# Key strips kept once per head, with zeros in the other heads' rows, for the scores of a causal attention stage

## The chip, the cores and the metric

The kernel runs on one NeuronCore of a Trainium2 chip. The metric is the device time of one execution in microseconds. PE is TensorE's matmuls, PEld its weight loads, DVE is VectorE, ACT is ScalarE, POOL is GpSimd, SP is SyncE.

## The reference

Four stages, each followed by a residual and a layer norm over 128 features, on x of 4 x 512 x 128 float32: a retention layer, two windowed attention layers with feed-forward, a causal attention layer, and a gated feed-forward of four matrix products. The change touches the causal stage alone:

```python
k = einsum('bte,fe->btf', x, Wk).reshape(B, T, 16, 8)    # q and v alike
k = layernorm(k, kln_g, kln_b); q = layernorm(q, qln_g, qln_b)   # over the 8 values of a head
dot = einsum('bihd,bjhd->bhij', q * s, k * s)
dot = where(causal, -inf, dot)
att = softmax(dot, axis=-1)
out = einsum('bhij,bjhd->bihd', att, v).reshape(B, T, 128)
return einsum('bte,fe->btf', out, Wo) + bo
```

## The kernel before, in words

All weights stay in SBUF. A hardware loop runs twice (`Fori(0, 2)`), and each turn does the four stages on two of the four sequences of 512 positions (8 tiles of 128 tokens; `G = 8`, `NT = 4`). Each engine has its own program, written out in order; semaphores join them, and nothing is planned at run time. PSUM's eight banks of 128 x 512 float32 are given out by `take`, which makes PE wait until the bank's last user is done.

**The causal stage.** A head has 8 values. Each of q and k is kept as a rounded high part and a low remainder, and these with two rows for the negated row maximum fill 32 slots for each head (`QS`, `KS`). Four heads make 128 slots. So the unit of work is `u`, 0 to 7: one of two sequences and one quad of heads. For each `u` PE transposes the four token tiles of `QS` and of `KS` (helper `transposes`, recorded at line 358) into bank 6, and ACT copies the bank out (helper `evac`, line 1227) as `qS[128, 512]` and `kS[128, 512]` in float32r: partition 32h + r is slot r of head h. These are the strips. `qS` and `qS2` have two buffers, `kS` has three.

- `first_pass` (line 628) makes scores with queries as the stationary operand: head n of pair p takes partitions 64p + 32n to + 32 of both operands, so a product contracts over 32 rows. Query tile t needs keys 0 to (t + 1) x 128. After the scores of two pairs, `masked` (line 615) adds the causal mask with a bf16 product of full width. DVE takes the row maxima of a bank pair (line 1114, `maxima`).
- `negated` writes the negated maxima into `QS`; PE transposes again, ACT copies to `qS2`. `second_pass` (line 647) makes transposed scores less the maximum, with keys as the stationary operand; ACT takes the exponential of a bank pair (line 1403), POOL clears the part above the diagonal (line 1575), and `values` (line 661) multiplies with v, 32 columns of the array for each head, into bank 7.
- `head_outputs` transposes the result (line 358), DVE divides (lines 1135, 1136), and later the output projection and layer norm follow (`finish`, line 682).

The stage is a loop over 24 steps and a tail (`for s in range(END)`). Step 3u + i makes group i of the first pass of unit `u` (`A_GROUPS`: 512 columns a head; 128 + 384; 256) and group i of the second pass four steps later (`B_GROUPS`, the same widths). A group has two fills, one for each pair of heads, and a fill takes one of three bank pairs. A fill of the second pass so waits for `maxima` to free its pair, or for the exponential. `k_strips(u + 1)` stands last in step 3u + 2, after `head_outputs`; step 3u + 3 opens with `first_pass` of unit u + 1, which waits for `kS_ready`. Both use bank 6.

`table2` holds the rotary tables of the windowed layers (2048 float32 for each partition). DVE writes it in `tables`, in the retention stage of each turn, and reads it last in the second windowed layer, where `swapped_ready` comes to 32.

**Ahead of the loop.** POOL waits for a DMA, casts a mask (line 1590), and enters the loop, where its first work is an addition over x (line 1498). ACT waits for `zeros_ready` and enters the loop, where its first work is the copy of the transposed x to `x_features`. PE's first products (line 376) need that copy.

Of the kernel before, what the change touches and what calls it, by code (L numbers as in the profile page):

```python
# [15 lines left out]
F32 = mybir.dt.float32  # L16
F32R = mybir.dt.float32r
# [4 lines left out]
P = 128  # L22
S = 512
NT = 4
G = 8
D = 128
H1, K1, V1 = 16, 8, 16
H2, D2, WIN = 8, 64, 64
# [37 lines left out]
def build(nc, x, wts, rows, consts, out):  # L66
    with ExitStack() as ctx:
        def sb(name, shape, dt=F32):
            return ctx.enter_context(nc.sbuf_tensor(name, shape, dt))

        def sem(name):
            return ctx.enter_context(nc.semaphore(name))
# [5 lines left out]
        xM = sb("x_tokens", [P, G, D])  # L78
        xi = sb("x_inner", [P, G, D])
        hT = sb("x_features", [P, 2, S + 1])  # L80
        table2 = sb("rotary2", [P, 2, 2, NT, 2, D2])
        band_bf = sb("band_bf", [P, 2, P], BF16)
        ident_bf = sb("ident_bf", [P, P], BF16)
        neghalf = sb("neghalf", [P, 1])
# [4 lines left out]

        qS = sb("q_strips", [P, 2, S], F32R)  # L90
        qS2 = sb("q_strips_shifted", [P, 2, S], F32R)
        kS = sb("k_strips", [P, 3, S], F32R)
        later_bf = sb("later_bf", [P, P], BF16)
        gb3 = sb("gain_bias3", [P, 512])
        neg3 = sb("negmax3", [P, 16], F32R)

        ARENA = 21200
        STAGING = 19600
        arena = sb("arena", [P, ARENA])

        def carve(sizes):
            offs, end = offsets(sizes)
            assert end <= ARENA, end
            return {k: arena[:, a:a + w] for k, (a, w) in offs.items()}
# [85 lines left out]
        psum = [banks[:, 512 * i:512 * i + 512] for i in range(8)]  # L190
# [9 lines left out]
        zeros_ready = sem("zeros_ready")  # L200
        masks_loaded = sem("masks_loaded")
        masks_ready = sem("masks_ready")
        arrived = sem("arrived")
        go = sem("go")
        settle = sem("settle")
# [3 lines left out]
        def counter(name):  # L209
            s = sem(name)  # L210
            cleared.append(s)
            return s
# [35 lines left out]
             "negmax_ready", "pe_qS2", "qS2_ready", "pe_B", "E_ready", "pe_V", "oS_ready", "pe_oS", "oN_ready",  # L248
             "pe_oN", "oNT_ready", "pe_wo3", "z3_ready"))
        xb3_ready = counter("xb3_ready")  # L250
        hi_placed = counter("hi_placed")
        kept3 = counter("kept3")

# [20 lines left out]
        def held(key):  # L274
            return psum[place[key]]
# [19 lines left out]
        A_GROUPS = [[(3, 0)], [(0, 0), (2, P)], [(1, 0)]]  # L295
# [6 lines left out]
        def fill_of(f):  # L302

            return f // NF, f % NF // 2, f % 2
# [50 lines left out]
        def _(pe):  # L355
# [217 lines left out]
            def causal():  # L573
# [32 lines left out]
                def next_pair(key, until):  # L606
                    i = filled[0] % 3
                    filled[0] += 1
                    for n in range(2):
                        take(pe, (key, n), until, bank=2 * i + n)  # L610
                    place[key] = i
                    return i
# [5 lines left out]
                def first_pass(fills):  # L618
                    for f in fills:
                        u, group, p = fill_of(f)  # L620
                        if f % NF == 0:
                            pe.wait_ge(qS_ready, u + 1)
                            pe.wait_ge(kS_ready, u + 1)
                        i = next_pair(("A", f), [(mx_ready, f + 1)])
                        for n in range(2):
                            rows = slice(64 * p + 32 * n, 64 * p + 32 * n + 32)
                            for t, at in A_GROUPS[group]:
                                pe.matmul(psum[2 * i + n][:, at:at + (t + 1) * P], qS[rows, u % 2, t * P:(t + 1) * P],  # L628
                                          kS[rows, u % 3, 0:(t + 1) * P], start=(at == 0), stop=False,
                                          skip_group_check=True)  # L630
                    for f in fills:
                        u, group, p = fill_of(f)
                        for n in range(2):
                            for t, at in A_GROUPS[group]:
                                mm = masked(psum[2 * place["A", f] + n], at + t * P)
                        mm.then_inc(pe_A, 1)

                def second_pass(fills):
                    for f in fills:
                        u, group, p = fill_of(f)  # L640
                        if f % NF == 0:
                            pe.wait_ge(qS2_ready, u + 1)
                        i = next_pair(("B", f), [(E_ready, f + 1)])
                        for n in range(2):
                            rows = slice(64 * p + 32 * n, 64 * p + 32 * n + 32)
                            for t, at in B_GROUPS[group]:
                                mm = pe.matmul(psum[2 * i + n][:, at:at + (NT - t) * P],  # L647
                                               kS[rows, u % 3, t * P:(t + 1) * P], qS2[rows, u % 2, t * P:S],
                                               start=(at == 0), stop=True, skip_group_check=True)
                        mm.then_inc(pe_B, 1)  # L650

# [39 lines left out]
                for s in range(END):  # L691
# [24 lines left out]
                    for k in HIDDEN_AT.get(s, ()):  # L716
                        i = filled[0] % 3
# [49 lines left out]
            with pe.Fori(0, 2) as it:  # L767
                retention()
                retention_end(pe)
                pe.wait_ge(consts_loaded[2], 16)  # L770
                pe.wait_ge(tables_ready, 1)
                for l in range(2):
                    pe.wait_ge(loaded[2 + l], 16)
                    if l == 0:
                        pe.wait_ge(pads_ready, 1)
                    window_layer(l)
                    gelu_layer(l)
                pe.wait_ge(strips_blank, 2)
                pe.wait_ge(masks_ready, 1)
                causal()  # L780
                mlp()
                pair_end(pe, it)
# [442 lines left out]
        def _(act):  # L1225
            def evac(dst, src):
                return act.activation(dst, src, ACT.Copy)  # L1227
# [124 lines left out]
            def causal():  # L1352
# [32 lines left out]
                def k_strips(u):  # L1385
                    act.wait_ge(pe_kS, u + 1)
                    if u >= 3:
                        act.wait_ge(pe_B, NF * (u - 2))
                    evac(kS[:, u % 3, :], held(("kS", u))[:]).then_inc(kS_ready, 1)

                def shifted_strips(u):
                    act.wait_ge(pe_qS2, u + 1)
# [61 lines left out]
            def mlp():  # L1454
# [17 lines left out]
            act.dma_start(C[:, CONST_CUTS[1]:CONST_CUTS[2]], consts[:, CONST_CUTS[1]:CONST_CUTS[2]])\  # L1472
                .then_inc(consts_loaded[1], 16)
            act.wait_ge(zeros_ready, 1)
            with act.Fori(0, 2) as it:
                retention()
                retention_end(act)
                act.wait_ge(pads_ready, 1)
                for l in range(2):
                    act.wait_ge(loaded[2 + l], 16)  # L1480
                    window_layer(l)
                    gelu_layer(l)
                causal()
                mlp()
                pair_end(act, it)
# [3 lines left out]
        def _(pool):  # L1489
# [66 lines left out]
                        root(LN2 + 2 * G + g)  # L1556

            def causal():
                pool.wait_ge(xM_ready, 2 * G)
                pool.tensor_tensor(xi[:], xM[:], r_("bo3").unsqueeze(1).to_broadcast([P, G, D]), ALU.add)\  # L1560
                    .then_inc(xb3_ready, 1)
                def affine(g):
                    pool.wait_ge(scaled3, g - NT + 1)
                    flat = cen3[:, g % NT].rearrange("p h d -> p (h d)")
                    pool.tensor_tensor(flat, flat, gb3[:, 0:256], ALU.mult).then_inc(affine_step, 1)
                    pool.wait_ge(affine_step, g - NT + 1)
                    pool.tensor_tensor(flat, flat, gb3[:, 256:512], ALU.add).then_inc(affine3, 1)

                def keep(f):

                    u, group, p = fill_of(f)
                    pool.wait_ge(E_ready, f + 1)
                    for t, at in B_GROUPS[group]:
                        diagonal = PT3[group][:, 2 * p:2 * p + 2, at:at + P]
                        ins = pool.affine_select(out=diagonal, in_=diagonal, pattern=[[0, 2], [1, P]],  # L1575
                                                 compare_op=ALU.is_ge, fill=0.0, base=0, channel_multiplier=-1)
                    ins.then_inc(kept3, 1)

                for s in range(END):
                    for g in SCALE_AT.get(s, ()):  # L1580
                        affine(g)
                    for f in fills_b(s):
                        keep(f)
                    if s in FINISHED_AT:
                        root(LN3 + FINISHED_AT[s])
                for g in range(NT, G):
                    root(LN3 + g)

            pool.wait_ge(masks_loaded, 16)
            pool.tensor_copy(later_bf[:],  # L1590
                             arena[:, STAGING:STAGING + MASKS_WIDTH]).then_inc(masks_ready, 1)
            pool.wait_ge(zeros_ready, 1)
            pool.wait_ge(rows_loaded[0], 16)
            with pool.Fori(0, 2) as it:
# [173 lines left out]
```

## Time and profile before

| | |
|---|---|
| median of 3 runs | 1305.03 us |
| the runs | 1286.44, 1307.96, 1305.03 us |
| profiled execution, its own time | 1297.12 us |
| span of the profiled execution | 1295.4 us |
| PE busy | 1031.7 us (80%) |
| DVE busy | 749.7 us (58%) |
| ACT busy | 542.9 us (42%) |
| POOL busy | 388.8 us (30%) |
| mean granted clock of TensorE | 0.856 |

The span is the time from the first to the last instruction of the profiled execution. Busy times are unions over an engine's instructions; the clock is a share of full speed, 1.0 being 2.4 GHz and 0.5 being 1.2 GHz.

### The profile page before, as it was taken

To read this page: it belongs to the slowest core of one execution; us is meant where nothing else is said; L and a number is where in the kernel's file an instruction comes from. 1 tells how busy PE (TensorE), PEld (TensorE's weight loads), DVE (VectorE), ACT (ScalarE), POOL (GpSimd) and SP (SyncE) were. 2 spreads that over 40 slices of the span, in tenths; PEclk is the share of its full clock that TensorE was granted. 3 is DMA by queue.
4 is the path that set the end of the run, shared out by engine and by line. 5 is a ranking of instruction groups with operands and counts; after the bars stand their busy time and mean duration, and the time that the engine had idled before them with its cause. 6 is when DMAs were issued, how large, how long until landed. Compare 5 with 4: busy or idle time off the path is not lost.

```text
span 1295.4 us, 18716 instructions
## 1 busy us (share of the span) xinstructions
PE 1031.7 (80%) x6640; PEld 638.7 (49%) x6640; DVE 749.7 (58%) x1906; ACT 542.9 (42%) x1066; POOL 388.8 (30%) x373
## 2 busy tenths in 40 slices
PE   6996688978884777899389957888788847877994
PEld 3665466645662444444246644566466523443443
DVE  4675578577867655330356746885887666443303
ACT  3730455445533554531065304553555335444410
POOL 2235445144441322200213444531443503122001
PEclk9876799989996698699787757999899956687997
DMA  8000000010000000000100001000100000000001
GB/s 334 2 1 0 22 17 22 1 25 13 22 1 1 1 2 1 1 1 1 34 2 1 1 1 25 18 18 1 25 22 14 1 1 1 2 1 1 1 1 32
DMA packets 11630, 21.61 MB, mean 17 GB/s; under 512 B 1424, under 2 KB 6928, under 8 KB 11024
## 3 DMA queue, kind: packets, MB, share of 16 engines
q1 hardware_dynamic: 11248, 18.60, 4.9%
q10 hardware_dynamic: 288, 1.79, 0.4%
q8 instruction: 56, 0.92, 0.3%
q14 instruction: 38, 0.31, 0.1%
HBM read 11.87 MB, written 1.05 MB: 10 GB/s over the span
## 4 chain that ended last, share of the span: by engine, by line
PE 64%; DVE 19%; issue 7%; ACT 5%; POOL 2%; POOLq 1%; DMA 1%; SPq 0%; DVEq 0%; ACTq 0%
PE bank L740 9%; PE bank L358 7%; PE bank L392 6%; PE bank L498 6%; PE bank L407 5%; PE bank L457 4%; PE bank L661 4%; DVE arena L1114 3%; PE bank L521 3%; PE bank L531 2%; DVE arena L970 2%; PE bank L730 2%; PE bank L628 2%; PE bank L647 2%; PE bank L492 2%
## 5 line engine op out<-in xcount | busy, mean ns | idle before, releaser
L1227 ACT ACTIVATE arena<-bank 128x512 f32<-128x512 f32 (+3 forms) x340 | 165.4, 528 | 263.5 <-PE bank L358 239.1
L358 PE MATMUL bank<-consts_sb,arena 128*128 128x128 f32 x960 | 154.0, 300 | 81.3 <-DVE arena L1106 26.7
L358 PEld LDWEIGHTS bank<-consts_sb,arena 128*128 128x128 f32 x960 | 116.4, 154 | 141.3 <-issue 57.6
L1114 DVE TENSOR_REDUCE arena<-bank 128x2 f32<-128x1024 f32 (+3 forms) x128 | 98.1, 819 | 105.3 <-PE bank L615 105.2
L1527 POOL TENSOR_TENSOR arena<-arena,neghalf 128x16 f32<-128x16 f32 x32 | 93.3, 2915 | 215.7 <-DVE arena L972 215.7
L1492 POOL TENSOR_TENSOR rstd<-vareps,neghalf 128x1 f32<-128x1 f32 x96 | 54.8, 571 | 260.1 <-DVE vareps L800 259.7
L1575 POOL TENSOR_SCALAR_AFFINE_SELECT arena<-arena 128x256 f32<-128x256 f32 x128 | 50.9, 411 | 226.5 <-ACT arena L1403 224.2
L740 PE MATMUL bank<-arena,weights 128*128 128x512 f32 x256 | 111.9, 594 | 1.6 <-ACT arena L1459 1.6
L457 PE MATMUL bank<-weights,x_features 128*128 128x512 f32 x192 | 94.2, 632 | 10.6 <-ACT x_features L1227 10.6
L1403 ACT ACTIVATE arena<-bank 128x1024 f32<-128x1024 f32 (+1 forms) x96 | 81.9, 881 | 48.7 <-PE bank L647 47.9
L392 PE MATMUL bank<-arena 128*128 128x512 f32 x128 | 79.1, 775 | 5.2 <-ACT arena L1251 5.1
L498 PE MATMUL bank<-arena 128*64 128x128 f32 x1024 | 78.2, 300 | 0.0
L740 PEld LDWEIGHTS bank<-arena,weights 128*128 128x128 f32 x256 | 48.0, 190 | 61.0 <-issue 57.4
L1251 ACT ACTIVATE arena<-arena,consts_sb 128x128 f32<-128x128 f32 x256 | 75.6, 396 | 0.0
L970 DVE TENSOR_REDUCE arena<-arena 128x16 f32<-128x1024 f32 x32 | 39.0, 1218 | 62.2 <-ACT arena L1285 62.2
L498 PEld LDWEIGHTS bank<-arena 128*64 128x64 f32 x1024 | 61.5, 150 | 17.2 <-issue 17.2
L407 PEld LDWEIGHTS bank<-arena 128*128 128x128 f32 x512 | 67.3, 212 | 3.2 <-issue 1.9
L1533 POOL TENSOR_TENSOR arena<-arena 128x1024 f32<-128x1024 f32 x28 | 66.0, 2357 | 0.0
L647 PE MATMUL bank<-q_strips_shifted,k_strips 32*128 32x512 f32 (+3 forms) x256 | 48.3, 450 | 22.1 <-DVE arena L1114 21.6
L407 PE MATMUL bank<-arena 128*128 128x17 f32 x512 | 65.6, 276 | 0.0
L1003 DVE TENSOR_REDUCE arena<-bank 128x4 f32<-128x512 f32 x64 | 44.0, 688 | 33.2 <-PE bank L498 31.5
L1459 ACT ACTIVATE arena<-bank,weights 128x512 f32<-128x512 f32 x32 | 22.0, 687 | 97.6 <-PE bank L740 97.6
(164 smaller groups left out, 1788.3 us busy)
## 6 DMA issues: line engine op xcount, KB each, us to landing
arena<-arena SPq DMA_DIRECT2D x56, 130.0 KB, 2.3
weights<-wts_dram SPq DMA_DIRECT2D x1, 2824.0 KB, 19.3
weights<-wts_dram SPq DMA_DIRECT2D x1, 1817.0 KB, 13.3
weights<-wts_dram SPq DMA_DIRECT2D x1, 1561.0 KB, 9.4
x_tokens<-x_dram SPq DMA_DIRECT2D x6, 256.0 KB, 3.0
consts_sb<-consts_dram ACTq DMA_DIRECT2D x1, 1232.5 KB, 7.1
out_dram<-x_inner SPq DMA_DIRECT2D x16, 64.0 KB, 1.5
consts_sb<-consts_dram SPq DMA_DIRECT2D x1, 768.0 KB, 4.6
```

The source lines that it names most:

```text
L358: mm = pe.transpose(bank[:, i * P:(i + 1) * P], src, ident)
L392: pe.matmul(bank[:], kT1[:, b, t * P:(t + 1) * P], qx1[g % 2][:, 4 * c:4 * c + 4, :], start=True, stop=True).then_inc(pe_sc, 1)
L407: mm = pe.matmul(bank[:, 17 * h:17 * h + 17], PT1[:, g % 2, h, :], v1[:, g, h, :], start=(t == 0 and h == 0), stop=(h == H1 - 1), skip_gro ...
L457: pe.matmul(bank[:], hT[:, b, t * P:(t + 1) * P], w_(f"qkv2_{l}")[:, 512 * j:512 * j + 512], start=True, stop=True).then_inc(done, 1)
L498: mm = pe.matmul(bank[64 * w:64 * w + 64, i * P:(i + 1) * P], qT2[:, g % 2, h // 2, 64 * w:64 * w + 64], kz[:, g % 2, h, 64 * w:64 * w + P ...
L647: mm = pe.matmul(psum[2 * i + n][:, at:at + (NT - t) * P], kS[rows, u % 3, t * P:(t + 1) * P], qS2[rows, u % 2, t * P:S], start=(at == 0), ...
L740: mm = pe.matmul(bank[:], w_(name)[:, 512 * c + k * P:512 * c + (k + 1) * P], src[:, b, c, :], start=(c == 0), stop=(c == 3))
L1114: ins = dve.tensor_reduce(mx3[:, u % 2, t, 2 * p:2 * p + 2], scores[:, :, at:at + (t + 1) * P], AX, ALU.max)
L1227: return act.activation(dst, src, ACT.Copy)
L1251: ins = act.activation(qx1[g % 2][:, h, :], qT1[:, b, t * P:(t + 1) * P], ACT.Copy, scale=c_("headmask")[:, h:h + 1])
L1403: act.activation(PT3[group][:, 2 * p:2 * p + 2, 0:wide], pair_view(place["B", f])[:, :, 0:wide], ACT.Exp).then_inc(E_ready, 1)
L1527: pool.tensor_tensor(rn2[:, g % 2, :], ss2[:, g % 2, :], neghalf[:].to_broadcast([P, 16]), ALU.pow).then_inc(rn_ready, 1)
```

## The change

The keys' strips are stored four times, `kS[128, 3, 4, 512]`. Copy h holds head h's 32 rows; the other 96 rows are zero. POOL clears buffers 0 and 1 once ahead of the loop and buffer 2 in each turn, since buffer 2 now lies on the memory of `table2`. ACT writes the copies with four activations of 32 partitions each instead of one of 128. Both passes then contract over all 128 rows: the query operand is the whole strip of four heads, and the zeros take the other heads out. In the first pass the loop over tiles is now the outer one and that over the two heads the inner one. The arena is 96 floats smaller.

```diff
-        kS = sb("k_strips", [P, 3, S], F32R)
+        at = nc.sbuf_base
+        kS = sb("k_strips", [P, 3, 4, S], F32R)
+        table2 = nc.alloc_sbuf_tensor_at("rotary2", [P, 2, 2, NT, 2, D2], F32, offset=at + 2 * 4 * S * 4)
...
                             pe.wait_ge(kS_ready, u + 1)
+                            if u == 2:
+                                pe.wait_ge(third_blank, 2)
                         i = next_pair(("A", f), [(mx_ready, f + 1)])
-                        for n in range(2):
-                            rows = slice(64 * p + 32 * n, 64 * p + 32 * n + 32)
-                            for t, at in A_GROUPS[group]:
-                                pe.matmul(psum[2 * i + n][:, at:at + (t + 1) * P], qS[rows, u % 2, t * P:(t + 1) * P],
-                                          kS[rows, u % 3, 0:(t + 1) * P], start=(at == 0), stop=False,
+                        for t, at in A_GROUPS[group]:
+                            for n in range(2):
+                                pe.matmul(psum[2 * i + n][:, at:at + (t + 1) * P], qS[:, u % 2, t * P:(t + 1) * P],
+                                          kS[:, u % 3, 2 * p + n, 0:(t + 1) * P], start=(at == 0), stop=False,
                                           skip_group_check=True)
...
                         for n in range(2):
-                            rows = slice(64 * p + 32 * n, 64 * p + 32 * n + 32)
                             for t, at in B_GROUPS[group]:
                                 mm = pe.matmul(psum[2 * i + n][:, at:at + (NT - t) * P],
-                                               kS[rows, u % 3, t * P:(t + 1) * P], qS2[rows, u % 2, t * P:S],
+                                               kS[:, u % 3, 2 * p + n, t * P:(t + 1) * P], qS2[:, u % 2, t * P:S],
...
                 pe.wait_ge(masks_ready, 1)
+                pe.wait_ge(keys_blank, 2)
                 causal()
...
-                    evac(kS[:, u % 3, :], held(("kS", u))[:]).then_inc(kS_ready, 1)
+                    if u == 2:
+                        act.wait_ge(third_blank, 2)
+                    for h in range(4):
+                        rows = slice(32 * h, 32 * h + 32)
+                        ins = evac(kS[rows, u % 3, h, :], held(("kS", u))[rows, :])
+                    ins.then_inc(kS_ready, 1)
...
             act.wait_ge(zeros_ready, 1)
+            act.wait_ge(keys_blank, 2)
             with act.Fori(0, 2) as it:
...
             def causal():
+                pool.wait_ge(swapped_ready, 4 * G)
+                pool.memset(kS[:, 2, :, :].bitcast(F32), 0.0)
+                pool.drain().then_inc(third_blank, 2)
                 pool.wait_ge(xM_ready, 2 * G)
...
                              arena[:, STAGING:STAGING + MASKS_WIDTH]).then_inc(masks_ready, 1)
+            pool.memset(kS[:, 0:2, :, :].bitcast(F32), 0.0)
+            pool.drain().then_inc(keys_blank, 2)
             pool.wait_ge(zeros_ready, 1)
```

## Rows read from the trace of the kernel before

**Rows 1.** The page, part 4: the chain of work that ended last, by engine.
```profile
PE 64%; DVE 19%; issue 7%; ACT 5%; POOL 2%; POOLq 1%; DMA 1%; SPq 0%; DVEq 0%; ACTq 0%
```

**Rows 2.** Causal stage: length, busy PE, PEld, DVE, ACT, POOL (count), PEclk, DMA share, GB/s.
```profile
411.78:556.86 145.08, 114.39 (x816) 60.25 (x817) 73.07 (x161) 72.37 (x117) 33.48 (x76) 0.80 0.00 1
1053.85:1207.37 153.52, 122.90 (x816) 63.96 (x816) 73.37 (x161) 72.61 (x117) 33.35 (x76) 0.72 0.00 1
```

**Rows 3.** PE, one unit in time: start, length, what, [idle before <-releaser].
```profile
457.51 0.62 PE L628 MATMUL bank<-k_strips,q_strips 32*128 32x512 f32 x4 [0.73 <-issue]
458.06 0.40 PE L615 MATMUL bank<-later_bf,ident_bf 128*128 128x128 bf16 x4
...
459.76 0.38 PE L647 MATMUL bank<-q_strips_shifted,k_strips 32*128 32x256 f32 x2 [0.54 <-DVE arena L1114]
460.07 1.07 PE L661 MATMUL bank<-arena 128*32 128x384 f32 x16
461.07 0.57 PE L628 MATMUL bank<-k_strips,q_strips 32*128 32x128 f32 x8
461.57 0.62 PE L615 MATMUL bank<-later_bf,ident_bf 128*128 128x128 bf16 x8
...
463.44 0.49 PE L647 MATMUL bank<-q_strips_shifted,k_strips 32*128 32x512 f32 x2 [0.82 <-DVE arena L1114]
463.87 0.64 PE L661 MATMUL bank<-arena 128*32 128x256 f32 x8
...
465.02 0.39 PE L628 MATMUL bank<-k_strips,q_strips 32*128 32x256 f32 x4
465.34 0.40 PE L615 MATMUL bank<-later_bf,ident_bf 128*128 128x128 bf16 x4
...
466.50 0.50 PE L647 MATMUL bank<-q_strips_shifted,k_strips 32*128 32x384 f32 x4 [0.33 <-DVE arena L1114]
```

**Rows 4.** All engines at the seam of two units.
```profile
456.12 0.66 PE L358 MATMUL bank<-consts_sb,arena 128*128 128x128 f32 x4 [0.68 <-DVE arena L1136]
456.81 0.60 ACT L1227 ACTIVATE k_strips<-bank 128x512 fp32r<-128x512 f32 x1 [1.44 <-PE bank L358]
```

**Rows 5.** Stretches: a unit at full clock, one mostly at half clock.
```profile
1123.62:1136.79 13.17, 10.06 (x98) 5.54 (x98) 7.12 (x13) 7.35 (x10) 3.18 (x8) 1.00 0.00 1
1105.32:1123.62 18.30, 16.56 (x97) 8.52 (x97) 7.12 (x13) 7.27 (x10) 3.17 (x8) 0.56 0.01 2
```

**Rows 6.** ACT, two copies of 64 partitions each from one bank, back to back.
```profile
132.51 1.20 ACT L1227 ACTIVATE x_features<-bank 64x512 f32<-64x512 f32 x2 [10.12 <-PE bank L358]
```

**Rows 7.** PE, float32 products of full width, after the causal stage.
```profile
556.86 10.57 PE L740 MATMUL bank<-arena,weights 128*128 128x512 f32 x24
```

**Rows 8.** Groups by line on POOL: clearing memory (busy us, mean ns).
```profile
L1598 POOL MEMSET arena<- 128x3072 f32 x2 | 5.3, 2658 | 1.0 <-DVEq L284 1.0
```

**Rows 9.** The start of the execution on POOL, ACT and PE.
```profile
9.67 0.29 POOL L1590 CAST later_bf<-arena 128x128 bf16<-128x128 f32 x1 [9.14 <-DMA arena<-consts_dram]
...
9.85 0.60 ACT L1227 ACTIVATE x_features<-bank 128x512 f32<-128x512 f32 x1 [6.67 <-PE bank L358]
...
10.59 2.77 PE L376 MATMUL bank<-x_features,weights 128*128 128x512 f32 x4
```

**Rows 10.** POOL and DVE as the causal stage opens.
```profile
393.22 2.34 POOL L1560 TENSOR_TENSOR x_inner<-x_tokens,rowconsts 128x1024 f32<-128x1024 f32 x1 [0.46 <-DVE x_tokens L805]
...
393.50 2.10 DVE L1072 TENSOR_SCALAR arena<-arena 128x32 f32<-128x32 f32 x1
```

**Rows 11.** PE in a unit whose clock falls shortly after 472.9, and the next unit's start.
```profile
470.65 0.62 PE L628 MATMUL bank<-k_strips,q_strips 32*128 32x512 f32 x4 [0.73 <-issue]
...
473.31 1.94 PE L661 MATMUL bank<-arena 128*32 128x384 f32 x16
...
485.30 0.62 PE L628 MATMUL bank<-k_strips,q_strips 32*128 32x512 f32 x4 [0.73 <-issue]
```

More of the change, by code:

```diff
@@ L80, in build @@
         hT = sb("x_features", [P, 2, S + 1])
-        table2 = sb("rotary2", [P, 2, 2, NT, 2, D2])
         band_bf = sb("band_bf", [P, 2, P], BF16)
@@ L95, in build @@
         neg3 = sb("negmax3", [P, 16], F32R)
-        ARENA = 21200
+        ARENA = 21104
         STAGING = 19600
@@ L202, in build @@
         masks_ready = sem("masks_ready")
+        keys_blank = sem("keys_blank")
         arrived = sem("arrived")
@@ L250, in build @@
         xb3_ready = counter("xb3_ready")
+        third_blank = counter("third_blank")
         hi_placed = counter("hi_placed")
```

## The prediction

> **What bounds the kernel now.** I read the chain of waits first: 64% of the span is PE, 19% DVE, only 5% ACT [rows 1]. Next the causal stage in each turn: 145.08 and 153.52 us, 298.6 together. PE is busy for 79% and 80% of it, at a mean granted clock of 0.80 and 0.72. The clock has two levels, 2.4 and 1.2 GHz, so twice the missing share is the time at 1.2: 58 + 86 = 144 us, 48% [rows 2]. Then one unit in time [rows 3]: PE goes from scores to mask, to transposes, to values, and waits for DVE's maxima three times (0.54, 0.82, 0.33 us) in the middle of a step and for ACT at the seam of two units. There PE transposes the keys at 456.12, ACT copies them from 456.81 for 0.60 us, and only at 457.51 do the scores of the next unit start [rows 4]. Nobody has other work there: PE idles 0.73, and ACT had idled 1.44 before. So whatever lengthens ACT's copy lengthens each unit by as much. A unit takes 13.17 us at full clock and 18.30 us at a clock of 0.56 [rows 5].
>
> **Term 1, the four copies.** One activation of 128 partitions becomes four of 32, each still 512 columns. No copy of 32 partitions is in the trace. The nearest rows are two of 64 partitions from one bank, 1.20 us for both [rows 6], against 0.60 for one of 128 [rows 4]: the time follows columns, not partitions. Bounds for the three added: 0 if they cost by partitions (4 x 0.15), 1.80 at 0.60 each. I take 1.80, since halving the partitions saved nothing. It comes 16 times, each on the path, unit 0 included, whose scores also wait for its strips: 16 x 1.8 = **+28.8 us**.
>
> **Term 2, the products.** Their number stays, 256 in each pass. Now four row groups run side by side: four products of 512 columns start at 457.51 and full-width work follows at 458.06, 0.55 later; 128 and 384 columns take 0.50 (461.07 to 461.57), 256 take 0.32 (465.02 to 465.34), 1.37 us for a unit's first pass. In the second pass only a pair stands together, and the second fill of a step is followed at once by the values: 0.31, 0.43, 0.43, which is 1.17 (the middle one at 463.44 to 463.87; the third, at 466.50, has as many columns and is taken as equal) [rows 3]. Between 256 and 512 columns lie 0.12 us, so 0.46 ns a column, near one column a cycle at 2.4 GHz (0.417), and about 0.2 us is a fixed part where a 32-row shape gives way to another.
> With 128 rows nothing runs side by side. Price of a column: float32r over 128 rows isn't in the trace. The float32 instruction of 512 columns takes 0.44 us (10.57 / 24) [rows 7], two cycles a column; the float32r ones of 32 rows take one. I take one, by the type; two is the far end. First pass: 4 x (512 + 128 + 384 + 256) = 5120 columns x 0.417 = 2.13 us, and no change of shape before the mask. So +0.77, +1.0 if the 128-column ones are held by weight loads; I take +0.8. Second pass: the first fill (+0.1 to 0.2) lies beside PE's waits for DVE and costs nothing while these last; at half clock they are gone. The second fill: 2560 columns, 1.07 us, and a change of shape to the values stays, 0.1 to 0.2 three times, so 1.37 to 1.67 against 1.17: +0.3. Together +1.1 a unit at full clock. At half clock the first pass's streaming doubles (4.27 against some 2.2), and of the second pass both fills show: +2.8. With 52% and 48%: 16 x (0.52 x 1.1 + 0.48 x 2.8) = **+31 us**, from 18 (all at full) to 45 (all at half).
>
> Two rules bear on this. The Trainium skill, TensorE: Matmul & The Clock Gate, Part 3: Packing small matmuls, speaks against the change: it gives 3.07 times the speed for four row groups at 512 columns. By it the four would take 0.28 us now instead of the 0.55 read above, and this term would be a few us larger. In TensorEngine Tiling, Key Properties, it says that changing the mode drains the engine, and the fixed 0.2 us of the rows agrees; with that cost the trace shows 0.85 / 0.55 = 1.5 times.
>
> **Term 3, the start.** POOL clears 4096 floats a partition after its cast, which ends at 9.96 [rows 9]. At 2658 / 3072 = 0.865 ns a float [rows 8] that is 3.5 us, to 13.5. ACT now waits for it before its first copy, at 9.85 before; behind that copy PE's first products (10.59) wait, and all else behind them [rows 9]. **+3.7 us**, once. POOL's own addition and what follows start as late as their inputs now do, so no more.
>
> **At nothing.** The clearing of the third buffer, 2048 x 0.865 = 1.8 us [rows 8], comes before POOL's addition at 393.22, which holds DVE for 2.10 us at its first small operation [rows 10]; both move together, and third_blank is asked for only at unit 2. If DVE is held later instead of at once: 0.5 us a turn. The new waits of PE are met long before. The arena and the loop order: nothing.
>
> **Term 4, the clock.** Half clock costs (18.30 - 13.17) / (0.88 x 18.30) = 0.32 us for each us at it [rows 5], so 144 us cost 46 us now. Two things pull apart. More columns stream in each unit (first pass 1.37 to 2.13, both fills of the second doubled), which keeps the clock up. But the seam's wait grows from 0.73 to 2.5 us, right after another wait of 0.68 and transposes of 0.66 [rows 4]; and a unit opened by such a seam fell to half clock even now (values at 473.31 took 1.94 us against 1.07 at 460.07) [rows 11, 3], and the unit 485.30 - 470.65 = 14.65 us against 13.17 [rows 11, 5]. I expect one such fall in nearly every unit, some 2 us with the longer wait, 16 x 2 = 32 instead of 46, and no long half-clock stretches: **-14 us**. Bounds: -46 (none), +30 (80% at half).
>
> **Sum.** 28.8 + 31 + 3.7 - 14 = +49.5 on the profiled execution's 1297: **1346 us**. That execution is 8 us under the median 1305, among runs from 1286 to 1308; against the median the forecast is +3.2%. About 2% is what a measurement of this kernel tells from no change.
>
> **Rivals.**
> - *The clock stays up.* Full-width work is denser, and the seam isn't enough to bring the clock down. Then 28.8 + 18 + 3.7 - 46 = +4: 1301, within 2%. For it: once the clock was up it stayed for units on end at PE 76% busy [rows 5]. Against it: the seam three times as long, sixteen times.
> - *Faster.* Place: the changes of array shape. Suppose that those before a 32-row product cost as much as those behind it, 0.2 us for each of its 7 groups on the path (three, one, three), so term 2 is not +1.1 but -0.3 a unit; with the full clock and copies at 0.48 spacing (1.4 a unit), 23 - 5 + 3.7 - 46 = -24: 1273, 2.5% under the median. It decides when the wait for the maxima does not take the gain. Against it: the first pass alone grows by 0.77 with that cost counted.
> - *Two cycles a column.* Another 2.13 + 1.07 = 3.2 us a unit, 51 us: 1397, less what a fuller PE gets back in clock, 1385.
> - *The clock sinks.* 80% at half: 28.8 + 39 + 3.7 + 30 = +101, 1398.
> - *It doesn't do what it says:* four products with one stationary operand might skip loads. Nothing in the code drops one, so no chance of its own.
>
> **How the numbers follow.** Forecast 0.62 (1320 to 1370), clock up 0.19, faster 0.06, two cycles 0.07, clock sinks 0.06. The range 1302 to 1382 leaves out the faster case, half of the clock case, half of the two dear ones. Slower by over 2% (above 1331): 0.57 of the forecast's 0.62 and the two dear ones, 0.70. Within: 0.24. Faster: 0.06.
>
> **What would show it.** ACT: 64 copies to the strips of 32 partitions, four of a unit 2.4 us long, and PE idle some 2.5 us before line 628's successor. Four products of 512 columns 0.85 us apart from the mask at full clock; 1.7 would be the two-cycle rival. PE's first full products at 14.3 instead of 10.59. A unit at full clock 16.1 us. The mean granted clock of the stage: 0.8 as forecast, 0.95 and more for the first rival. Wrong I would be if the copies overlap or cost by partitions (1317), or by the clock.

## The result and the profile after

The changed kernel takes **1349.97 us** (median, 1346.94 to 1352.43), the kernel before 1297.13 in the same comparison (1286.44 to 1307.96): a ratio of **1.0435, 95% interval 1.033 to 1.0539**. It is slower. 1346 was forecast. A ratio and its interval leave out runs over 1.5% above the fastest of the same kernel, among them the profiled one of experiment 2 (1371.12 us), whose median is given without it too.

The profiled execution took 1351.35 us, its span is 1349.6: 54.2 more than before. First the chain of work that ended last, by engine; "issue" is time in which the engine waited for nothing that the profile shows.

```profile
PE 63%; DVE 18%; issue 9%; ACT 5%; POOL 2%; POOLq 1%; SPq 0%; DMA 0%; DVEq 0%; ACTq 0%
```

Against [rows 1] only "issue" grew, from 7% to 9%. Next, as in [rows 2 and 5], the causal stage of the first turn, its second unit, the stage of the second turn, and one unit of it: length, busy PE, PEld, DVE, ACT, POOL with counts, granted clock, DMA share, GB/s.

```profile
420.39:592.38 171.99, 131.09 (x816) 84.13 (x816) 73.20 (x161) 84.71 (x138) 33.20 (x76) 0.83 0.00 1
437.42:460.64 23.22, 15.45 (x66) 10.09 (x67) 11.75 (x29) 9.72 (x15) 5.21 (x10) 0.65 0.00 1
1090.51:1261.53 171.02, 130.00 (x816) 83.09 (x817) 73.63 (x161) 84.87 (x138) 33.41 (x76) 0.83 0.00 1
1166.49:1184.11 17.62, 13.50 (x97) 8.92 (x97) 7.12 (x13) 9.03 (x13) 3.15 (x8) 0.89 0.00 1
```

The stages grew from 145.08 and 153.52 to 171.99 and 171.02, together by 44.4 of the 54.2 us. 8.6 lie ahead of the first scores (411.79 to 420.39), 1.1 between the stages. ACT's busy time in a stage rose by 12.3, PE's by 17 and 7, while the stages grew by 27 and 18; the rest is PE's waiting. The granted clock is higher than before: 0.83 against 0.80 and 0.72. It isn't even over the stage: the second unit has 0.65 and takes 23.22 us, the later ones about 0.89 and 17.6 to 17.8.

PE in time, from one seam of two units to the next (start, length, what, idle before and its releaser):

```profile
511.48 0.66 PE L363 MATMUL bank<-consts_sb,arena 128*128 128x128 f32 x4 [0.68 <-DVE arena L1142]
514.66 2.01 PE L634 MATMUL bank<-k_strips,q_strips 128*128 128x512 f32 x4 [2.52 <-issue]
516.47 0.65 PE L620 MATMUL bank<-later_bf,ident_bf 128*128 128x128 bf16 x4
...
518.72 1.07 PE L666 MATMUL bank<-arena 128*32 128x384 f32 x16
519.72 1.41 PE L634 MATMUL bank<-k_strips,q_strips 128*128 128x128 f32 x8
...
532.39 0.77 PE L634 MATMUL bank<-k_strips,q_strips 128*128 128x512 f32 x1 [2.52 <-issue]
```

Three things are to be seen. PE's idle time at the seam is 2.52 us where it was 0.73 [rows 4]. The four products of 512 columns hold PE from 514.66 to 516.47, 1.81 us, where they take 1.01 at full clock (experiment 1): the clock is at 1.2 GHz behind the wait. By 518.72 it is back at 2.4: the values take 1.07 us as in [rows 3], not the 1.94 of [rows 11]. The unit is 532.39 - 514.66 = 17.73 us long, against 13.17 at full clock before.

All engines as a stage opens: the four copies, and what POOL and DVE did before them.

```profile
398.01 0.34 DVE L811 TENSOR_SCALAR x_tokens<-x_inner,meanvar,rstd 128x128 f32<-128x128 f32 x1
...
398.71 1.80 POOL L1572 MEMSET k_strips<- 128x2048 f32 x1
398.79 1.79 DVE L811 TENSOR_SCALAR x_tokens<-x_inner,meanvar,rstd 128x128 f32<-128x128 f32 x1 [0.44 <-POOL rstd L1504]
...
400.69 2.34 POOL L1575 TENSOR_TENSOR x_inner<-x_tokens,rowconsts 128x1024 f32<-128x1024 f32 x1 [0.18 <-DVE x_tokens L811]
...
401.31 1.75 DVE L1078 TENSOR_SCALAR arena<-arena 128x32 f32<-128x32 f32 x1
...
404.44 0.23 DVE L1084 TENSOR_SCALAR arena<-arena 128x128 int32<-128x128 int32 x1
...
417.90 2.39 ACT L1233 ACTIVATE k_strips<-bank 32x512 fp32r<-32x512 f32 x4 [1.21 <-PE bank L363]
```

Four copies of 32 partitions take 2.39 us, 0.60 from one to the next, the price of a copy of 128 partitions [rows 4]. And the start, where [rows 9] stood:

```profile
9.71 3.51 POOL L1607 MEMSET k_strips<- 128x4096 f32 x1
...
13.49 1.28 ACT L1233 ACT_TABLE_LOAD   x1 [13.49 <-POOLq L1608]
13.73 2.35 POOL L1510 TENSOR_TENSOR x_inner<-x_tokens,rowconsts 128x1024 f32<-128x1024 f32 x1 [0.51 <-issue]
14.79 1.09 ACT L1233 ACTIVATE x_features<-bank 128x512 f32<-128x512 f32 x2
...
15.53 1.19 PE L381 MATMUL bank<-x_features,weights 128*128 128x512 f32 x1 [5.04 <-ACT x_features L1233]
```

PE's first products start at 15.53 instead of 10.59. The load of ACT's table, 1.28 us, now stands behind the wait for the clearing; in the kernel before it started at 1.89 us, long ahead of the first copy.

### The profile page after: what moved, and what is told of

It reads as the page before. It is cut to its first block, busy times and chain, and to the rows that moved or that the text cites. A ratio compares the mean times of both kernels' runs of the same rounds, so it can differ in the third digit from the quotient of the medians.

```text
span 1349.6 us, 18777 instructions
## 1 busy us (share of the span) xinstructions
PE 1051.8 (78%) x6640; PEld 679.2 (50%) x6640; DVE 751.7 (56%) x1906; ACT 570.1 (42%) x1114; POOL 395.2 (29%) x376
## 3 DMA queue, kind: packets, MB, share of 16 engines
q10 hardware_dynamic: 288, 1.79, 0.3%
## 4 chain that ended last, share of the span: by engine, by line
PE 63%; DVE 18%; issue 9%; ACT 5%; POOL 2%; POOLq 1%; SPq 0%; DMA 0%; DVEq 0%; ACTq 0%
PE bank L745 8%; PE bank L363 7%; PE bank L397 6%; PE bank L503 5%; PE bank L412 5%; PE bank L634 4%; PE bank L462 4%; PE bank L666 3%; DVE arena L1120 3%; PE bank L526 2%; PE bank L652 2%; PE bank L536 2%; DVE arena L976 2%; PE bank L735 2%; PE bank L497 2%
## 5 line engine op out<-in xcount | busy, mean ns | idle before, releaser
L363 PE MATMUL bank<-consts_sb,arena 128*128 128x128 f32 x960 | 150.9, 296 | 86.7 <-DVE arena L1112 31.7
L634 PE MATMUL bank<-k_strips,q_strips 128*128 128x512 f32 (+3 forms) x256 | 70.7, 419 | 35.5 <-issue 35.3
L652 PE MATMUL bank<-q_strips_shifted,k_strips 128*128 128x512 f32 (+3 forms) x256 | 65.5, 371 | 20.1 <-DVE arena L1120 20.0
L634 PEld LDWEIGHTS bank<-k_strips,q_strips 128*128 128x128 f32 x256 | 47.9, 237 | 45.1 <-issue 41.7
```

Of the source, the lines that this page charges most:

```text
L363: mm = pe.transpose(bank[:, i * P:(i + 1) * P], src, ident)
L634: pe.matmul(psum[2 * i + n][:, at:at + (t + 1) * P], qS[:, u % 2, t * P:(t + 1) * P], kS[:, u % 3, 2 * p + n, 0:(t + 1) * P], start=(at == ...
L652: mm = pe.matmul(psum[2 * i + n][:, at:at + (NT - t) * P], kS[:, u % 3, 2 * p + n, t * P:(t + 1) * P], qS2[:, u % 2, t * P:S], start=(at = ...
```

## Experiments

In all of them the causal stage alone differs, but for the one wait that the third moves (5, 8 and 9 have it moved too). Ratios are to the kernel before, run beside each. At the mark of 2% the verdicts on experiments 2, 3, 4 and 9 are unclear, though their intervals lie wholly on one side of 1: the sign is shown, the size less well. "Stage" below is the sum of both turns in the profiled execution; before it is 298.6, after 343.0. "Time at 1.2 GHz" is twice the share by which the granted clock (taken unrounded) misses 1.0, times the stage: 143 us before, 119 after.

**1. The change with one copy of the four.** The strips of heads 1 to 3 of each quad are never written, so their scores are left out of what is computed; every product runs with the full width and count.

```diff
-                    for h in range(4):
+                    for h in range(1):
                         rows = slice(32 * h, 32 * h + 32)
                         ins = evac(kS[rows, u % 3, h, :], held(("kS", u))[rows, :])
```

> The changed kernel with one of the four copies of the key strips (head 0's); the other three are left out, so three heads' scores are zero. Products, clearing and start as changed. Seam theory (ACT's copies lie on the path between two units, 3 x 0.60 us sixteen times, and the longer wait lets TensorE's clock fall): 1350 - 29 - about 8 for the clock = 1313 us. Product theory (the loss of products side by side makes most of the 53 us): 1345 to 1350.

1301.4 us, ratio 1.0013 (0.9975 to 1.0051), stage 294.05. All of the loss goes with three copies of 0.6 us; it is below even the 1313 that the theory of the seam had. The stages and a unit (columns as above):

```profile
419.73:568.18 148.45, 116.99 (x817) 74.08 (x817) 73.22 (x161) 72.43 (x117) 33.22 (x76) 0.94 0.00 1
1063.92:1209.52 145.60, 114.76 (x816) 72.81 (x816) 72.98 (x161) 72.31 (x117) 33.33 (x76) 0.95 0.00 1
468.87:483.83 14.96, 12.03 (x97) 7.79 (x97) 7.12 (x13) 7.38 (x10) 3.16 (x8) 1.00 0.01 2
```

With full-width products and a short seam the clock stays up, 0.94 and 0.95: only 32 us at 1.2 GHz against 143. (The zeros that three heads now multiply are not what holds the clock up: experiment 9, with all four copies, has 0.95 and 0.96.) And here the products can be read at full clock, PE in time:

```profile
472.97 1.41 PE L634 MATMUL bank<-k_strips,q_strips 128*128 128x128 f32 x8
474.22 0.62 PE L620 MATMUL bank<-later_bf,ident_bf 128*128 128x128 bf16 x8
...
476.09 0.70 PE L652 MATMUL bank<-q_strips_shifted,k_strips 128*128 128x512 f32 x2 [0.73 <-DVE arena L1120]
476.73 0.64 PE L666 MATMUL bank<-arena 128*32 128x256 f32 x8
...
477.71 0.72 PE L634 MATMUL bank<-k_strips,q_strips 128*128 128x256 f32 x4
478.27 0.40 PE L620 MATMUL bank<-later_bf,ident_bf 128*128 128x128 bf16 x4
...
483.83 1.17 PE L634 MATMUL bank<-k_strips,q_strips 128*128 128x512 f32 x4 [0.72 <-issue]
484.84 0.40 PE L620 MATMUL bank<-later_bf,ident_bf 128*128 128x128 bf16 x4
```

Four products of 512 columns take 1.01 us to the mask's start (0.55 before), the mixed group of 128 and 384 takes 1.25 (0.50), that of 256 takes 0.56 (0.32): 2.82 a unit against 1.37. The unit is 14.96 against 13.17.

**2. The kernel before with its copy cut in four.** Products of 32 rows as before, nothing else of the change.

```diff
-                    evac(kS[:, u % 3, :], held(("kS", u))[:]).then_inc(kS_ready, 1)
+                    for h in range(4):
+                        rows = slice(32 * h, 32 * h + 32)
+                        ins = evac(kS[rows, u % 3, :], held(("kS", u))[rows, :])
+                    ins.then_inc(kS_ready, 1)
```

> The kernel before, with its one copy of the key strips made as four activations of 32 partitions each; products of 32 rows, nothing else changed. Seam theory: a unit goes from 13.17 to 15.0 us at full clock, 16 x 1.8 = 29 us, and the longer wait costs some more in clock: 1326 to 1336 us. Product theory: 1297 to 1302. If the clock falls after every seam as in the changed kernel, the mean granted clock of the causal stage is under the 0.76 of before, else not.

1338.09 us (1336.19 to 1351.76), ratio 1.0278 (1.0169 to 1.0387), just above the 1326 to 1336 of the seam theory. The copies alone make some 37 to 41 us of the 53, two thirds to three quarters of the loss. PE in time at a seam:

```profile
493.69 0.92 PE L628 MATMUL bank<-k_strips,q_strips 32*128 32x512 f32 x4 [2.52 <-issue]
```

The same wait of 2.52 us. The one profile is of the 1371 us execution, so its lengths and its clock are not set against the other kernels. What the three shorter runs have is a mean granted clock of their whole span, 0.842, 0.843 and 0.819, against 0.874 to 0.878 in the changed kernel's. An estimate of the stages from this: a span of 1336.4 us at 0.842 has 422 us at 1.2 GHz, and outside the causal stages every profiled execution has 221 to 233; so some 195 us of some 335 lie in the stages, against 119 of 343 after the change. So behind the same wait the kernel with products of 32 rows spends more time at 1.2 GHz than the one with products of 128.

**3. The change, ACT's wait for the cleared strips moved** from ahead of the loop to the first copy that needs it.

```diff
+                    if u == 0:
+                        act.wait_ge(keys_blank, 2)
...
                     for h in range(4):
...
-            act.wait_ge(keys_blank, 2)
             with act.Fori(0, 2) as it:
```

> The changed kernel with ACT's wait for the cleared strips moved from ahead of the loop to its first copy into them. In the changed trace PE's first products start at 15.53 instead of 10.59 us, since ACT's table load stands behind the wait too. Start theory: the whole 4.9 us come back, 1345 us. Rival (the later start is hidden in the retention stage, and something else made the causal stage open later): 1349 to 1350.

1345.27 us (1343.95 to 1346.59), ratio 1.0302 (1.0227 to 1.0376), 4.7 less than after, stage 343.04, the same. PE in time at the start:

```profile
10.45 4.31 PE L381 MATMUL bank<-x_features,weights 128*128 128x512 f32 x5
```

From 15.53 back to 10.45: the start costs about 5 us, by the medians and by the trace.

**4. The kernel before with the keys' strips made earlier in the step**, on PE ahead of the second pass, on ACT ahead of the exponentials. If the seam is what counts, taking it off the path must pay in the kernel before too.

```diff
+                    if s in K_AT:
+                        k_strips(K_AT[s])
...
-                    if s in K_AT:
-                        k_strips(K_AT[s])
```

> The kernel before, with the transposes of the next unit's keys moved from the end of a step to ahead of its second pass, and ACT's copy ahead of the exponentials. Seam theory: the wait of 0.73 us and the wait of 0.68 ahead of the transposes merge or go, at least 1.0 us a unit sixteen times, and the clock falls less often: 1265 to 1280 us. Rival (the path then runs through the exponentials, which start 0.6 us later in that step, and the maxima): 1290 to 1300.

1268.82 us (1266.06 to 1270.24), ratio **0.9711 (0.9639 to 0.9782)**: faster than the kernel before and the changed one. The stages and a unit:

```profile
411.77:549.25 137.48, 114.01 (x817) 59.84 (x817) 72.65 (x161) 72.20 (x117) 33.10 (x76) 0.76 0.01 1
1046.79:1180.32 133.53, 109.36 (x817) 57.80 (x817) 72.49 (x161) 71.88 (x117) 33.18 (x76) 0.81 0.01 1
456.30:467.28 10.98, 9.71 (x99) 5.32 (x98) 7.12 (x13) 6.88 (x10) 2.10 (x6) 0.99 0.01 3
```

PE and ACT in time at what was the seam:

```profile
465.11 0.65 PE L647 MATMUL bank<-q_strips_shifted,k_strips 32*128 32x384 f32 x8
465.22 0.60 ACT L1227 ACTIVATE k_strips<-bank 128x512 fp32r<-128x512 f32 x1 [0.26 <-PE bank L358]
...
466.69 0.66 PE L358 MATMUL bank<-consts_sb,arena 128*128 128x128 f32 x4
...
467.28 0.51 PE L628 MATMUL bank<-k_strips,q_strips 32*128 32x512 f32 x4
```

ACT copies while PE does the second pass, and the scores follow the last transposes without a gap. The unit is 10.98 us against 13.17.

**5. The same move, with experiment 3, in the changed kernel.**

> The changed kernel with the late wait for the cleared strips and the key transposes and copies ahead of the second pass. Seam theory: the four copies (2.39 us) lie beside the second pass and the values, a unit goes from 17.6 to about 13 us and no longer falls to half clock; 1345 - 70 = 1275 us. Rival (the copies only move the wait: the exponentials behind them start 1.9 us later and hold the next unit's bank pairs): 1310 to 1330.

1299.26 us, ratio 1.0066 (1.0036 to 1.0096), stage 296.9. Above the 1275 of the seam theory, below the rival's 1310: both missed. That is 46 us less than experiment 3, but the copies aren't hidden. A unit, then ACT and PE:

```profile
478.06:491.64 13.58, 11.84 (x99) 7.69 (x98) 7.11 (x13) 9.11 (x14) 3.16 (x8) 1.00 0.01 1
488.79 2.39 ACT L1233 ACTIVATE k_strips<-bank 32x512 fp32r<-32x512 f32 x4 [0.26 <-PE bank L363]
...
491.20 1.94 ACT L1416 ACTIVATE arena<-bank 128x1024 f32<-128x1024 f32 x2
491.23 0.66 PE L363 MATMUL bank<-consts_sb,arena 128*128 128x128 f32 x4 [0.38 <-ACT k_strips L1233]
```

PE still waits 0.38 for the copies (both users share bank 6), and the exponentials start only behind them.

**6. Experiments 2 and 4 together** (products of 32 rows, four copies, made early).

> The kernel before with the copy split in four (as in e2) and the key transposes and copies ahead of the second pass (as in e4). Seam theory: with the copies off the path their number hardly counts, 1269 to 1285 us, against 1336 to 1352 for the split copy at the seam. Rival (the exponentials queue behind the copies): 1295 to 1310.

1290.89 us, ratio 0.998 (0.9935 to 1.0025): again between the two forecasts, 22 above experiment 4. It is also 8 us below experiment 5, which has the same four early copies and products of 128 rows (1.0066, 1.0036 to 1.0096): the intervals don't meet.

**7. The change with only its second pass back on 32 rows.**

```diff
+                            rows = slice(64 * p + 32 * n, 64 * p + 32 * n + 32)
...
-                                               kS[:, u % 3, 2 * p + n, t * P:(t + 1) * P], qS2[:, u % 2, t * P:S],
+                                               kS[rows, u % 3, 2 * p + n, t * P:(t + 1) * P], qS2[rows, u % 2, t * P:S],
```

> The changed kernel with the second pass back on 32 rows (head h's own rows of its copy), the first pass on 128 rows. If full-width products help only by keeping the clock up: fewer columns stream, the clock falls more often than in the changed kernel (mean 0.826 in the stage), a unit at full clock is 0.5 us shorter: 1345 to 1365 us. If the second pass's width is a plain loss: 1335 to 1342.

1345.32 us (1340.93 to 1351.79), ratio 1.043 (1.0362 to 1.0497). At the lower edge of one range; against after, 4.7 us less with overlapping runs. So the medians don't decide what the second pass's width costs. The trace says a little more: a unit takes 17.2 us (after: 17.6 to 17.8), and the stages' clock is 0.84 and 0.86, not below the 0.83 of after, as the first forecast had it. In this one execution the second pass's width did not hold the clock up.

**8. Experiment 5 with one copy of four** (the same heads left out as in experiment 1).

> As e5, with one of the four copies and the other three left out, so three heads' scores are zero. A unit at full clock was 14.97 us with one copy at the seam; 2.2 less as in the kernel before with early keys: 12.8, and nearly no half clock: 1262 us. Against e5 it prices the copies beside the second pass: nothing by the seam theory, 1262 against 1275 at most; 30 us or more by the rival.

1276.76 us, ratio 0.988 (0.9827 to 0.9934). Against experiment 5 three copies cost 22.5 us beside the second pass, as much as between 4 and 6: 1.4 a unit instead of 3. In the profiled executions a unit at full clock takes 12.89 here and 13.58 in experiment 5, 0.7 apart, so the other half lies in units below full clock and in the stage's ends. Against experiment 4, which differs by the width of the products and the added clearings, this kernel is 8 us slower, and the intervals don't meet. The 1262 expected was missed by 15.

**9. Experiment 3 with PE kept at work during the wait.** Eight bf16 products of 512 columns ahead of the wait for `kS_ready`; their bank is overwritten by the scores. PE's wait for the bank pair has to stand ahead of them.

```diff
+                        i = next_pair(("A", f), [(mx_ready, f + 1)])
                         if f % NF == 0:
+                            for _ in range(8):
+                                pe.matmul(psum[2 * i].rearrange("p (h j) -> p h j", h=4), ident_bf[:],
+                                          band_bf[:, 1:2, :].to_broadcast([P, 4, P]),
+                                          start=True, stop=True, skip_group_check=True)
...
                             pe.wait_ge(kS_ready, u + 1)
...
-                        i = next_pair(("A", f), [(mx_ready, f + 1)])
```

> The changed kernel with the late wait, and eight more bf16 products of 512 columns on PE while it waits for the key copies (1.7 us of a wait of 2.5 at full clock; their result is overwritten). The copies stay at the seam. Clock theory (part of what the four copies cost is the half clock that follows the wait): a unit goes from 17.6 to 14.97 + 1.8 = 16.8 us, the half-clock time of the stage from 119 to under 60 us, total 1345 - 15 = 1330 us. Rival (the clock falls for another reason, or the extra products cost what they save): 1345 or more.

1324.16 us (1322.11 to 1324.80), ratio 1.0203 (1.0133 to 1.0273); units of 16.80 us. Its first stage:

```profile
415.24:576.18 160.94, 127.32 (x875) 77.81 (x874) 73.43 (x163) 85.17 (x138) 33.42 (x76) 0.96 0.00 1
```

And PE at one of its seams:

```profile
462.25 0.66 PE L363 MATMUL bank<-consts_sb,arena 128*128 128x128 f32 x4 [0.68 <-DVE arena L1146]
462.74 1.89 PE L629 MATMUL bank<-band_bf,ident_bf 128*128 128x512 bf16 x8
465.47 1.15 PE L638 MATMUL bank<-k_strips,q_strips 128*128 128x512 f32 x4 [0.84 <-ACT k_strips L1237]
```

From the transposes' end to the scores lie 2.56 us, where PE's idle time was 2.52 before, but the clock stays up (0.96 and 0.95 against 0.83), and 21 us come back in the medians and 22 in the stages (321.4 against 343.0). The ratios, each to its own runs of the kernel before, lie closer, 1.0203 and 1.0302, with overlapping intervals. This splits the copies' cost in two.

**10. The kernel before with three such products at each seam.**

> The kernel before with three more bf16 products of 512 columns in the wait of 0.73 us at the seam (0.65 us at full clock, 1.3 at half). Clock theory: units at half clock grow rarer, the stage's 143 us at half clock shrink by half, worth about 20 us at 0.32, less up to 0.6 us in each unit that is still at half clock: 1280 to 1290 against 1299. Rival (three products are too few, or hold up PE while it is slow): 1299 to 1308.

1301.55 us, ratio 1.002 (0.9977 to 1.0064): nothing gained, as the rival had it. The stage still shows 130 us at 1.2 GHz of 143. PE has no idle time left at the seam in this trace, so with products of 32 rows filling it did not keep the clock up. The clock was low in the first units of the first stage (0.74, 0.72, 0.69) and at its end (0.73).

## Why the prediction was right, step by step

Medians in us and ratios, with the copies, their place and the width of the products crossed:

| | one copy, at the seam | four, at the seam | one, early | four, early |
|---|---|---|---|---|
| products of 32 rows | 1297 to 1301 (before) | 1338, 1.028 (experiment 2) | 1269, 0.971 (4) | 1291, 0.998 (6) |
| products of 128 rows | 1301, 1.001 (experiment 1) | 1350, 1.044 (after); 1345, 1.030 (3) | 1277, 0.988 (8) | 1299, 1.007 (5) |

**The sum: near, with luck in it.** On the profiled executions +49.5 was forecast and +54.2 measured. Copies 28.8, start 4.9 and 1.6 for POOL's clearing (below) leave 18.9 for the products and the clock together, where the forecast had 31 - 14 = 17.

**Term 1, the copies: right.** 0.60 us each, 2.39 for four, PE idle 2.52 at each seam, as forecast. 16 x 1.8 = 28.8 us; experiment 9 shows it with the clock held up: 16.80 - 14.96 = 1.84 a unit. Not all that the copies cost is in this term: between experiment 1 and after lie 48.6 us, and experiment 9 gets 21 of them back by the clock alone.

**Term 3, the start: undersized.** 4.9 us instead of 3.7. The clearing took 3.51 as worked out; what I missed is the table load of 1.28 us, which before ended at 3.17, ahead of the first copy, and now waits too. Experiment 3 takes the whole term away.

**Term 2, the products: undersized at full clock.** +1.8 a unit, not +1.1. The first pass grew by 1.45 instead of 0.8: a column doesn't go at 0.417 ns but at 0.49 in products of 512 (1.01 us for 2048), 0.55 in those of 256, and 0.61 in the group with 128-column ones. The shorter the products, the dearer the column; that the weight loads between them are the reason is likely, but no run tests it. The group with the 128-column ones takes 1.25 instead of 0.85; the prediction named 0.2 us more for it as possible and took almost none of it. The second fills grew from 1.17 to 1.73 (0.40 + 0.64 + 0.69) instead of to 1.5. PE's waits for DVE gave back 0.15 (1.69 to 1.54). With both terms a unit at full clock was forecast at 16.1 us; experiment 9 has 16.80. One cycle a column was right, the two-cycle rival wrong: 1.7 us would have stood where 1.01 stands. With the change of shape behind them counted, the ratio to four row groups side by side is 1.01 / 0.55 = 1.8 and not the 1.5 of the prediction, still short of the 3.07 that the Trainium skill gives (TensorE: Matmul & The Clock Gate, Part 3: Packing small matmuls).

**Term 4, the clock: near in size, for half of the reasons.** A fall behind every seam is what happened, but each is cheap: a unit at 0.89 has 2 x 0.11 x 17.62 = 3.9 us at 1.2 GHz, and it takes 17.62 where experiment 9, with the clock up, takes 16.80. That is 0.8 us of cost where I had put 2. Even sixteen of them make only 62 of the 119 us at 1.2 GHz. The rest are the long stretches that I had ruled out, in the first units of a stage (0.65 over 23.22 us) and at its end. With the products at 16 x 1.8 = 29, the 18.9 above say that the clock gave back 10 where I had 14; the stages alone say the same (44.4, less 1.8 at each of the 14 seams inside them, leaves 19). That the products' 31 is so near to 29 is luck: it was 18 at full clock, filled up by 2.8 us for each unit at half clock, which no run measured by itself.

What the forecast didn't see is how the parts hang together. The rival "the clock stays up" was held unlikely because of the seam, and that was its true condition: with one copy the clock does stay up, and the product change costs nothing (1.0013), 29 us of columns paid by 110 us less at 1.2 GHz. The four copies then cost twice, 29 us of waiting and some 20 of clock. Had they been free, this kernel would have been a draw, not a gain. And the draw holds only at the seam: with the strips made early, products of 128 rows are 8 us behind those of 32 with one copy and with four, 1.6 of it the clearing of the third buffer (below), though their clock is higher (0.94 and 0.90 in experiment 8, 0.76 and 0.81 in experiment 4).

**At nothing: not quite.** I had the clearing of the third buffer move together with POOL's addition and its hold on DVE. The trace shows two holds, 1.79 us beside the clearing and 1.75 beside the addition, where one of 2.10 stood [rows 10]. What they cost can be read between DVE's last operation on `x_tokens` and its first on int32, in the kernel before:

```profile
392.79 0.35 DVE L805 TENSOR_SCALAR x_tokens<-x_inner,meanvar,rstd 128x128 f32<-128x128 f32 x1 [0.44 <-POOL rstd L1492]
...
397.64 0.23 DVE L1078 TENSOR_SCALAR arena<-arena 128x128 int32<-128x128 int32 x1
```

These are 4.85 us, and after the change 5.65 (398.79 to 404.44): 0.8 a turn, 1.6 in all, where 0.5 a turn was named as possible. From there to the first scores it is 14.15 before and 15.95 after, the 1.8 of unit 0's copies. So the 8.6 us by which the first scores come later are 0.8, 1.8, 4.9 from the start, and 1.1 that arose in the three stages between. That last part differs from one execution to the next: DVE's operation at 392.79 comes at 393.49 in experiment 3 and at 399.94 in experiment 1, so nothing of it can be laid to the change. The edits to the arena, the loop order and PE's new waits show no cost of their own.

## What to carry to other kernels

Before an operation is split or repeated, look where it stands: a copy with nobody else at work costs its full length each time, and on PE's side it can also cost the clock behind it. The first question about such a seam is whether it can be moved beside other work; in the kernel as it was that took 2.9% off the time (0.9639 to 0.9782), while the change around it lost 4.4%. Here a denser product paid for itself through the clock at a short seam, was not to be told from the other at a long one (1.030 and 1.028), and lost where the seam's work had been moved away. So measure the parts apart, and again together with the change that you mean to keep.

## What the runs showed of the hardware

- Copies of 32 partitions took as long as copies of 128: 0.60 us for 512 columns each.
- Products of 32 rows and of 128 rows differ in what they do for the clock. With one copy and a seam's wait of 0.72 to 0.73 us they left 143 and 32 us of the stages at 1.2 GHz (0.80 and 0.72; 0.94 and 0.95). With the same wait of 2.52 us the granted clock over the whole span was 0.819 to 0.843 with 32-row products (experiment 2), 0.874 to 0.878 in the changed kernel.
- Eight products of full width in the wait kept the clock at 0.96 and 0.95 where it was 0.83; three at a wait of 0.73 us, among products of 32 rows, left 130 us at 1.2 GHz of 143 and the time as it was (1.002).
- DVE's operation on 128 x 128 elements took 1.79 us while POOL cleared 2048 floats a partition, against 0.34 for the same operation just before (at 398.01): it ended at 400.58, right behind the clearing (400.51). The Trainium skill (SBUF — State Buffer, Who interferes with whom) names `tensor_scalar` among the operations that can block in whole behind one of POOL; this row agrees.
